# Transformer block with a mixture of experts on one core: no unused product beside the early logits, and the logits and first ranks of four blocks one group sooner

## What is computed

```python
x = x + lru(layernorm(x))                     # a diagonal linear recurrence
x = x + ffn_block(layernorm(x))

def ffn_block(x):
    h = x + attention(rmsnorm(x, ln1_w))      # 16 heads of 8, softmax over 1024 keys
    return h + moe(rmsnorm(h, ln2_w))

def moe(x):                                   # 8 experts, the best 2 for each token
    logits = x @ gate_w.T
    rw, sel = top_k(logits, 2)
    rw = softmax(rw)
    for e in range(8):
        we = sum(where(sel == e, rw, 0))
        out += (silu(x @ w1[e].T) * (x @ w3[e].T)) @ w2[e].T * we
```

## Time and profile before

| what | value |
|---|---|
| median of 3 runs (lowest, highest) | 1007.23 us (1007.21, 1008.69) |
| profiled execution, its own time | 1007.67 us |
| its span, first to last instruction | 1005.9 us |
| mean granted TensorE clock | 0.968 |
| busy: PE, DVE, ACT, POOL | 86%, 85%, 69%, 40% |

### The profile page before, as it was taken

One profiled execution on the slowest core, in us unless ns is written; L12 is line 12 of the kernel. 1 busy time (PEld: TensorE's weight loads), 2 busy tenths in 40 slices (PEclk: granted clock), 3 DMA queues, 4 the chain that ended last, 5 costly groups with the idle time before them and its releaser, 6 DMA issues.

```text
span 1005.9 us, 18290 instructions
## 1 busy us (share of the span) xinstructions
PE 867.5 (86%) x5968; PEld 361.7 (36%) x5968; DVE 854.6 (85%) x1463; ACT 690.2 (69%) x1471; POOL 400.4 (40%) x621
## 2 busy tenths in 40 slices
PE   0377788999999999999999999999999999989990
PEld 0155541222222223222222322222322246588990
DVE  4978889999999998988999898898799976768663
ACT  2614313888888888888888888888788875555660
POOL 7224441011010153533615443363577503346774
PEclk9789996999999999999999999999999999999995
DMA  9997643011010110100101010110101021122346
GB/s 313 387 362 192 165 111 90 9 26 28 13 25 10 32 25 9 46 9 26 38 25 25 9 46 10 33 46 10 24 31 39 18 48 48 44 63 69 105 145 198
DMA packets 60829, 74.34 MB, mean 74 GB/s; under 512 B 9152, under 2 KB 39104, under 8 KB 60352
## 3 DMA queue, kind: packets, MB, share of 16 engines
q1 hardware_dynamic: 53936, 62.93, 21.4%
q0 software_dynamic: 4608, 9.58, 2.8%
q10 hardware_dynamic: 2192, 0.66, 0.3%
HBM read 28.09 MB, written 44.79 MB: 72 GB/s over the span
## 4 chain that ended last, share of the span: by engine, by line
PE 60%; DVE 25%; ACT 7%; issue 5%; ACTq 1%; POOL 1%; DMA 1%; POOLq 0%; DVEq 0%; SPq 0%
PE ps L1634 21%; DVE nmax L1203 13%; PE ps L1624 10%; PE ps L1522 9%; PE ps L1736 7%; ACT prob L961 6%; PE ps L1752 3%; PE ps L1511 3%; PE ps L1697 2%; POOL by_token L810 1%; DVE wk L1153 1%; ACTq L836 1%; PE ps L1657 1%; PE ps L1716 1%; PE ps L1498 1%
## 5 line engine op out<-in xcount | busy, mean ns | idle before, releaser
L1203 DVE TENSOR_REDUCE nmax<-ps 128x1 f32<-128x1024 f32 x512 | 601.8, 1219 | 43.9 <-PE ps L1522 39.5
L961 ACT ACTIVATE prob<-ps 128x512 f32<-128x512 f32 x1024 | 529.6, 604 | 90.6 <-PE ps L1624 89.0
L1522 PE MATMUL ps<-packs 50*128 50x512 bf16 x1024 | 343.0, 389 | 9.7 <-DVE nmax L1203 5.4
L1624 PE MATMUL ps<-packs 50*128 50x512 bf16 x1024 | 312.1, 384 | 30.2 <-ACT prob L961 20.8
L1634 PE MATMUL ps<-prob,vpad 128*32 128x512 f32 x2048 | 273.6, 606 | 0.0
L1522 PEld LDWEIGHTS ps<-packs 50*128 50x128 bf16 x1024 | 74.8, 94 | 240.4 <-DVE nmax L1203 184.9
L1624 PEld LDWEIGHTS ps<-packs 50*128 50x128 bf16 x1024 | 75.9, 94 | 144.8 <-ACT prob L961 94.1
L544 POOL MEMSET packs<- 2x2048 bf16 x32 | 57.5, 1796 | 171.1 <-PE ps L1624 169.9
L810 POOL DMA_INDIRECT by_token<-wk,vall x80 | 80.1, 1001 | 96.1 <-DVE wk L1293 61.4
L1736 PE MATMUL ps<-ws 128*128 128x128 f32 x640 | 87.2, 280 | 2.9 <-DVE ws L1313 2.1
L1736 PEld LDWEIGHTS ps<-ws 128*128 128x128 f32 x640 | 78.6, 193 | 8.7 <-issue 7.0
(11 more groups left out here) (300 smaller groups left out, 857.8 us busy)
## 6 DMA issues: line engine op xcount, KB each, us to landing
by_expert_rows<-prob SPq DMA_DIRECT2D x4, 5016.0 KB, 36.8
packs<-k_parts SPq DMA_DIRECT2D x32, 192.0 KB, 3.6
packs<-q_parts SPq DMA_DIRECT2D x64, 96.0 KB, 3.1
vall<-by_expert_rows SPq DMA_DIRECT2D x80, 66.0 KB
packs<-by_token SPq DMA_DIRECT2D x8, 512.0 KB, 5.4
w<-w_t SPq DMA_DIRECT2D x3, 1024.0 KB, 10.7
q_parts<-front SPq DMA_DIRECT2D x16, 192.0 KB, 3.1
k_parts<-front SPq DMA_DIRECT2D x16, 192.0 KB, 3.4
```

The costliest lines, as they stand in the source:

```text
L961: act.activation(prob[:, v % RING, :], bank(col_bank(pos)), ACT.Exp).then_inc(col_free, 1)
L1203: dve.tensor_reduce(nmax[:, half, par, pair, qt:qt + 1], bank(first, 2), AX_X, ALU.max, negate=True).then_inc(row_free, 1)
L1522: ins = pe.matmul(bank(first + kh), qpack[r:r + ROWS, slot, half, pair, qt * P:(qt + 1) * P], kpack[r:r + ROWS, slot, pair, kh * HALF:(kh ...
L1624: pe.matmul(bank(col_bank(pos)), kpack[r:r + ROWS, slot, head // 2, kt * P:(kt + 1) * P], qpack[r:r + ROWS, slot, half, head // 2, :], sta ...
```

## The change

Two things are changed. The product of L1668 is left out in all six blocks that had it. For blocks 0 to 3, `logits` moves from the end of group 5, where it stood behind `m_own`, to the end of group 4, where nothing stood; and `prefix` moves from the end of group 9, where it stood ahead of `totals`, to the end of group 8, where nothing stood but ACT's `save_o`. `turn_h`, `totals`, and all the places of blocks 4 and 5 stay.

```diff
         FRONT_STEPS = ("turn_a", "project", "turn_h", "logits", "prefix", "totals")
-        FRONT_AT = {t: ((2 * t + 4, 7), (2 * t + 4, 9), (2 * t + 5, 3), (2 * t + 5, 5), (2 * t + 5, 9), (2 * t + 5, 9))
+        FRONT_AT = {t: ((2 * t + 4, 7), (2 * t + 4, 9), (2 * t + 5, 3), (2 * t + 5, 4), (2 * t + 5, 8), (2 * t + 5, 9))
                     for t in range(4)}
         FRONT_AT[4] = ((12, 4), (12, 6), (12, 12), (12, 13), (13, 1), (13, 1))
@@
                 elif name == "logits":
-                    if not late:
-                        pe.matmul(out[:, HALF // 2:HALF], ident[:, :], flat13[:, 0:HALF // 2],
-                                  start=True, stop=True, skip_group_check=True)
                     for k in range(4):
                         ins = pe.matmul(out[:, k * NE:(k + 1) * NE], h_T[:, k * P:(k + 1) * P], wgate[:, :],
                                         start=(k == 0), stop=True, skip_group_check=True)
```

## The result

| | before | after |
|---|---|---|
| median of 12 runs (lowest, highest), us | 1009.01 (1007.19, 1010.42) | 1007.14 (1005.41, 1008.03) |
| ratio after/before, 95% interval | | 0.9977 [0.997, 0.9984] |
| profiled execution: own time, span, us | 1007.67, 1005.9 | 1007.44, 1005.7 |
| mean granted clock | 0.968 | 0.966 |

The change makes the kernel faster by 2.3 us by the ratio (1.6 to 3.0), 1.9 by the medians. The predicted gain of 2.80 lies inside that interval. The time is not the predicted one: 1007.14 is 2.7 above 1004.4 and 1.1 above the range, while the kernel before, run twelve times, has a median 1.8 above the one that the forecast started from.

A forecast was written before the change was run, and what follows sets the result against it. No single engine bounds the kernel, but PE sets the pace in the changed groups. 4 x (0.36 + 0.12) + 0.88 = 2.80 us gain; 1004.87 from the profiled 1007.67, 1004.4 from the median; range 1003.0 to 1006.0.

The forecast's parts named there:

- the level: Starting time of the whole kernel: median of the runs shown, 0.44 us below the profiled 1007.67, making the forecast 1004.4.
- Rival 3: Clock beside the experts: without the low stretch 1003.0, 8%; one more, there or in the attention, 1005.8, 6%.
- The unused product: All six blocks: leaving it out gives back 0.44 us each, bounds 0.32 and 0.63.
- The rival of 0.22: Six blocks: each product gives back 0.22 us, not 0.44, as the skill's formula gives; 1005.7, chance 2%.
- The logits alone: Group 4, blocks 0 to 3: as only item they cost 1.00 us (0.79 to 1.10), making the group 3.65.
- The splitting: Groups 4 and 5: separating the logits from `m_own` costs some 0.08 us of the product's 0.44.
- `prefix` and `totals` apart: Groups 8 and 9: together 5.51 us against 5.63, a gain of 0.12 for each of four blocks.
- The copy of `prefix`: ACT, groups 8 and 9: stays covered, first exponential 0.47 us into group 9; uncovered, the pair loses 0.12.
- Rival 1: Groups 4, 8, 9: copy of `prefix` late and uncovered, logits cost as much as `project`; gain 1.2 us, 1006.0; 13%.
- POOL with `hot`: Group 8: `prefix` waits for POOL's `hot`, which is done with 2.2 us to spare.
- Rival 4: Group 8: POOL late with `hot`, PE stands at `prefix`; costs 4 x (x - 2.2) us for lateness x; 4%.
- Blocks 4 and 5 "only lose the product": Blocks 4 and 5, places unchanged: gain 2 x 0.44 = 0.88 us, with POOL moving with PE.

## Why the prediction was wrong, and what of it was right

- **The step that failed is the level.** It said: "the median of the runs shown is 0.44 lower, and from it the forecast is 1004.4". The twelve runs of before lie at 1007.2 (three), 1008.7 to 1009.1 (six) and 1010.3 to 1010.4 (three), 1.4 to 1.8 apart; the three shown held two of the lowest. From the median of twelve the same sum gives 1006.2, which misses by 0.9. So 1.8 of the miss of 2.7 is the level, and the rest lies within the interval of the measured gain (1.6 to 3.0, for 2.80 predicted). The forecast allowed the level nothing.
- **Rival 3 was put in the wrong place.** The clock was priced beside the experts and, against the odds, in the attention. Beside the experts it did as before (last weighing to end 127.17 and 127.05). The price there was too low: counting MATMULs gave 1.4, while the clock of the earlier trace rows gives (0.38 + 0.47) x 2 = 1.70. Where it differs is the recurrence, which the prediction never looked at because the change doesn't touch it: 1.70 us for each low stretch beside L1498, near the steps between the run times. That these steps are such stretches is an inference; only single executions have a trace. The mean granted clock, which every run has, supports it: of the changed kernel's twelve runs the four shortest (1005.41 to 1006.54) have 0.966 and the three longest (1007.50 to 1008.03) 0.964, and 1.70 us are 0.0017 of the span. In the unchanged kernel's 35, 23 and 18 runs on the other chips, too, the longer a run the lower its clock (correlations of -0.60, -0.69 and -0.72). That speaks for the clock, not for the place. The page "TensorE: Matmul & The Clock Gate" of the Trainium skill (section "What's actually happening") says that the chip's watch on activity runs freely and doesn't start with the kernel. The three profiles of the unchanged kernel, with the first weighing at 171.47, 171.41 and 173.30, would fit that, but they come from three chips and do not show it.
- **The unused product**, 0.44: right, 0.43 where it was the only edit. The rival of 0.22 is out.
- **The logits alone**, 1.00: right, 0.99, and group 4 is 3.64. The splitting was said to cost 0.08 of it; it costs nothing, because `m_own` alone behind the weighing is 0.05 and group 5 2.45, not 2.51. `m_next` in group 13, from which 2.51 was taken, is no equal: the term was 0.06 too large.
- **`prefix` and `totals` apart**, 0.12: right, 0.13 on every chip. The copy of `prefix` stayed covered (0.45 into the group, 0.47 said). Rival 1 is out.
- **POOL with `hot`**, 2.2 us to spare: right, 2.13. Rival 4 is out.
- **Blocks 4 and 5 "only lose the product", 2 x 0.44**: the one term of the sum with a size that is far off. Block 4 gives 0.43; block 5 gave 0.04 in the profile. The prediction let POOL move with PE; in quad 13 POOL was held by its own scatters and did not move. The error of 0.4 was mostly made up for by the 0.08 more in each of the four blocks, chiefly the split that cost nothing. So it is partly luck that the sum of 2.80 stands so near the 2.62 of the touched groups, and nearer still to the milestones' 2.86, of which 0.13 is not the change's.

## What to carry to other kernels

An absolute forecast needs the level as well as the gain. Look at the spread of many runs of the kernel before, not at the median of three. Ask also in which stretches, though the change never touches them, the clock can still differ. Where two traces are compared, measure from a milestone behind the last untouched stage.

When an engine gains on others, ask of each partner whether it is paced by the engine that moved or by its own queue. Only the first moves along.

## What of the hardware was not expected

- The granted clock differs between executions at unchanged places: the eight f32 products of L1498 took 3.70 or 6.76 us in profiles of one program (from different chips), and 5.40 in others, all behind the same gap of 1.11.
- An f32 product of 256 columns costs 0.43 to 0.44 us in a row of others and shows 0.63 on the chain when it stands first behind the weighing.
- Other chips ran the same program in 1061 to 1066 us instead of 1009, with all engines standing at fixed places, some of them beside bursts of indirect scatters (group 15 of quad 5: 5.78 us against 2.40) and in the experts' stage: from the last weighing to the end 164.3 us against 127.2. What they wait for no row names, and what stands in the experts' stage was not looked into.
